# Padding the slots of a split adjacency matrix and the blocks of its features by 32 bytes in a float32r graph kernel

## The chip, the core and the metric

The kernel runs on one core of a Trainium2 chip. The metric is the device time of one execution, in microseconds. Before the change it is 406.56 us, the median of three runs (406.36 to 406.57).

## The reference

`N` is 4096 nodes and `D` is 128 features. Two branches share one adjacency matrix `adj` (4096 x 4096, float32):

```
h   = relu(layernorm(x))                      # 4096 x 128
for (feat, eps, W, b) in ((h, eps1, W1, b1), (x2, eps2, W2, b2)):
    ax = adj @ feat
    y  = ax + (1 + eps) * ax
    for i in range(3):
        y = relu(y @ W[i].T + b[i])
out = x + concat(y1, y2) @ Wm.T + bm
```

Nearly all of the arithmetic is in the two products with `adj`.

## The kernel before

**Split operands.** TensorE is given float32r operands. To keep float32 accuracy each operand is split into a high part (a rounded copy) and a low part (what the rounding lost). A product is then three matmuls into the same PSUM bank: low features with high adjacency (L587), high features with high adjacency (L588), high features with low adjacency (L591). The features are the stationary operand (128 columns, loaded by LDWEIGHTS), and the adjacency is the moving operand (512 columns). The function `product` writes this, and `aggregate` and `opening_aggregate` call it for every block. The first units of the kernel use `passes` (L605) and `norm_aggregate` (L633, L638) for the same three products in another order, and the branch of `x2` uses plain float32 matmuls on unsplit data for its first two units (L619).

**Tiling.** The output is made in 8 chunks of 512 columns. A chunk needs 8 units of the adjacency. A unit is 128 partitions by 2048 columns, which are 4 blocks (`j`) of 512 columns (2048 bytes) each. A unit is used for both branches: 4 blocks x 2 branches x 3 matmuls are 24 matmuls. There are 64 units in all.

**Staging.** `adj_raw`, `adj_hi` and `adj_lo` are rings of 4 slots; unit `u` of a chunk stands in slot `u % 4`. SyncE's queue loads a unit of 1 MB into `adj_raw`, ScalarE copies it to `adj_hi` (L277), VectorE subtracts to make `adj_lo` (L447), and TensorE reads `adj_hi` and `adj_lo`. Units are fed back by the semaphore `unit_used`. The features are split once, in the opening (L319, L343 and L353 on ScalarE for `feat_hi`, L246 and L253 on GpSimd for `feat_lo`), and stay in `feat_hi` and `feat_lo`, [128, 2 branches, 32 blocks, 128], for the whole kernel.

**Layers.** Between the units of a chunk TensorE does the layers of the chunk before (`branch_layer`, `merge`), again with `product`: the stationary operand is a block of `w_lo` or `w_hi`, the moving operand is `act_hi` or `act_lo`. Their output goes to `hidden` and `merged`. The last chunk's late branch does its layers in quarters, with plain float32 (L733, L739).

**Order.** The order on each engine is written out by hand, program loops included; no planner and no pool decides it. Tensors take SBUF in the order in which they are declared, each start rounded up to 32 bytes.

**Where operands start.** The build places `adj_hi` at byte 49280, `adj_lo` at 82048, `feat_hi` at 114816, `feat_lo` at 147584, `w_hi` at 201152, `w_lo` at 205248, `act_hi` at 213600 and `act_lo` at 217696 of each partition. `adj_raw` (16512) and `x2_rows` (188544), the operands of the plain float32 matmuls, stand beside them. Counted modulo 512 bytes (a stationary block is 128 x 4 = 512 bytes long), every block of the adjacency, split or raw, and every block of the features and of `x2_rows` begins at 128, every block of `w_hi` and `w_lo` at 448, and both halves of `act_hi` and `act_lo` at 96.

Of the kernel before, what the change touches and what calls it, by code (L numbers as in the profile page):

```python
# [6 lines left out]
def gnn_layer_kernel(nc, adj_tiles, adj_first, adj_second, x_tiles, x2_tiles, x_t, w_t, bias_t, eps, out_t):  # L7
# [3 lines left out]
    F32R = mybir.dt.float32r  # L11
# [8 lines left out]
    CHUNKS = N // CW  # L20
    U = UNITS_ALL // CHUNKS
    BLOCKS = N // P
    RING = 4
    LAYERS = 3
    STEPS = LAYERS + 1
# [45 lines left out]
    with ExitStack() as ctx:  # L71
# [8 lines left out]


        adj_raw = sb("adj_raw", [P, RING, UNIT_COLS])
        adj_hi = sb("adj_hi", [P, RING, UNIT_COLS], F32R)
        adj_lo = sb("adj_lo", [P, RING, UNIT_COLS], F32R)

        feat_hi = sb("feat_hi", [P, 2, BLOCKS, D], F32R)
        feat_lo = sb("feat_lo", [P, 2, BLOCKS, D], F32R)

        x_rows = sb("x_rows", [P, X_SLOTS, JB, D])
# [74 lines left out]
        def f32(ap):  # L164
            return ap.bitcast(F32)
# [73 lines left out]
        @block.gpsimd  # L239
        def _(pool):  # L240

            def low_of_x2(u):
                rows = slice(u * JB, (u + 1) * JB)
                pool.wait_ge(x2_loaded[u % X_SLOTS], 16 * (u // X_SLOTS + 1))
                pool.wait_ge(feat2_hi_made, x2_count(u))
                nc.gpsimd.tensor_tensor(feat_lo[:, 1, rows, :], x2_rows[:, u % X_SLOTS], f32(feat_hi[:, 1, rows, :]),  # L246
                                        ALU.subtract).then_inc(feat2_lo_made, 1)

            def low_of_x(u):
                rows = slice(u * JB, (u + 1) * JB)  # L250
                pool.wait_ge(feat1_hi_made, u + 1)
                pool.wait_ge(relu_made, u + 1)
                nc.gpsimd.tensor_tensor(feat_lo[:, 0, rows, :], x_rows[:, u % X_SLOTS], f32(feat_hi[:, 0, rows, :]),  # L253
                                        ALU.subtract).then_inc(feat1_lo_made, 1)

            low_of_x(0)
            for u in range(1, U):
                low_of_x2(u)
                low_of_x(u)
                if u == 1:  # L260
                    low_of_x2(0)
            pool.dma_start(x_res[:, :], x_t[:, 0:CW]).then_inc(res_loaded, 16)


            with pool.Fori(0, CHUNKS - 1) as c:
                pool.wait_ge(y_made, c + 1)
                pool.dma_start(out_t[:, bass.ds(c * CW, CW)], y_sb[:, :]).then_inc(out_stored, 16)  # L267
                pool.wait_ge(out_stored, 16 * (c + 1))
                pool.dma_start(x_res[:, :], x_t[:, bass.ds(c * CW + CW, CW)]).then_inc(res_loaded, 16)
            pool.wait_ge(out_stored, 16 * (CHUNKS - 1))  # L270

        @block.scalar
        def _(act):
            def high_of_unit(c, u):
                act.wait_ge(raw_loaded[u % RING], 16 * (c * (U // RING) + (u // RING + 1)))
                act.wait_ge(unit_used, c * U + (u + 1 - RING))
                nc.scalar.activation(adj_hi[:, u % RING, :], adj_raw[:, u % RING, :], ACT.Copy).then_inc(hi_made, 1)  # L277

            def source(m, k, b):

# [30 lines left out]
            def high_of_opening(s):  # L311
                act.wait_ge(raw_loaded[s % RING], 16 * (s // RING + 1))
                if s >= RING:
                    act.wait_ge(unit_used, s + 1 - RING)
                nc.scalar.activation(adj_hi[:, s % RING, :], adj_raw[:, s % RING, :], ACT.Copy).then_inc(hi_made, 1)  # L315

            def high_of_x2(u):
                act.wait_ge(x2_loaded[u % X_SLOTS], 16 * (u // X_SLOTS + 1))
                nc.scalar.activation(feat_hi[:, 1, u * JB:(u + 1) * JB, :], x2_rows[:, u % X_SLOTS],  # L319
                                     ACT.Copy).then_inc(feat2_hi_made, 1)  # L320

            def std_of_x(u):
# [12 lines left out]
            def rectify_half(h, rectified, rounded):  # L335

                blocks = slice(h * HALF, (h + 1) * HALF)
                for j in range(blocks.start, blocks.stop):
                    xs = x_rows[:, 0, j, :]
                    last = nc.scalar.activation(xs, xs, ACT.Relu, bias=shift[:, j:j + 1], scale=rstd[:, j:j + 1])  # L340
                last.then_inc(rectified, 1)
                act.wait_ge(rectified, 1)
                nc.scalar.activation(feat_hi[:, 0, blocks, :], x_rows[:, 0, blocks, :], ACT.Copy).then_inc(rounded, 1)  # L343

            def rectify(u):

                act.wait_ge(rstd_made, u + 1)
                for j in range(JB):
                    xs = x_rows[:, u % X_SLOTS, j, :]
                    last = nc.scalar.activation(xs, xs, ACT.Relu, bias=shift[:, j:j + 1], scale=rstd[:, j:j + 1])  # L350
                last.then_inc(relu_made, 1)
                act.wait_ge(relu_made, u + 1)
                nc.scalar.activation(feat_hi[:, 0, u * JB:(u + 1) * JB, :], x_rows[:, u % X_SLOTS],  # L353
                                     ACT.Copy).then_inc(feat1_hi_made, 1)


# [77 lines left out]
        def _(dve):  # L434
# [8 lines left out]
            def low_of_unit(c, u):  # L443
                dve.wait_ge(raw_loaded[u % RING], 16 * (c * (U // RING) + (u // RING + 1)))
                dve.wait_ge(hi_made, c * U + (u + 1))
                dve.wait_ge(unit_used, c * U + (u + 1 - RING))
                nc.vector.tensor_tensor(adj_lo[:, u % RING, :], adj_raw[:, u % RING, :], f32(adj_hi[:, u % RING, :]),  # L447
                                        ALU.subtract).then_inc(lo_made, 1)

            def low_of_branch(m, k, b):  # L450
# [51 lines left out]
            def low_of_opening(s):  # L502
                dve.wait_ge(raw_loaded[s % RING], 16 * (s // RING + 1))
                dve.wait_ge(hi_made, s + 1)
                if s >= RING:
                    dve.wait_ge(unit_used, s + 1 - RING)
                nc.vector.tensor_tensor(adj_lo[:, s % RING, :], adj_raw[:, s % RING, :], f32(adj_hi[:, s % RING, :]),  # L507
                                        ALU.subtract).then_inc(lo_made, 1)

            nc.vector.memset(zero[:, :], 0.0).then_inc(zero_made, 1)  # L510
# [72 lines left out]
        def _(pe):  # L583
# [16 lines left out]
            def passes(out, s, b, passes_of, start=False):  # L600
                u = OPENING[s][0]
                for k, (feat, adj) in enumerate(passes_of):
                    for j in range(JB):
                        slot, cols = columns(s, j)
                        last = nc.tensor.matmul(out[:, :], feat[:, b, u * JB + j, :], adj[:, slot, cols],  # L605
                                                start=start and k == 0 and j == 0, stop=False)
                return last

# [14 lines left out]
            def norm_aggregate():  # L623

                for h in range(2):
                    pe.wait_ge(feat1_hi_made if h else half_feat1_made, 1)
                    for s in range(2):
                        out = opening_bank(s, late)
                        whole = s == 0 or h == 1
                        pe.wait_ge(hi_made if whole else fine_hi_made, s + 1 if whole else SECOND_UNIT + 1)  # L630
                        for j in range(h * HALF, (h + 1) * HALF):
                            slot, cols = columns(s, j)
                            nc.tensor.matmul(out[:, :], feat_hi[:, late, j, :], adj_hi[:, slot, cols],  # L633
                                             start=(j == 0), stop=False)
                        pe.wait_ge(lo_made if whole else fine_lo_made, s + 1 if whole else SECOND_UNIT + 1)
                        for j in range(h * HALF, (h + 1) * HALF):
                            slot, cols = columns(s, j)
                            nc.tensor.matmul(out[:, :], feat_hi[:, late, j, :], adj_lo[:, slot, cols],  # L638
                                             start=False, stop=False)
                pe.wait_ge(feat1_lo_made, 1)  # L640
                for s in range(2):
                    signal(0, late, passes(opening_bank(s, late), s, late, [(feat_lo, adj_hi)]))
# [20 lines left out]
            def opening_aggregate(s, b):  # L663
# [5 lines left out]
                pe.wait_ge(feat2_lo_made if b else feat1_lo_made, u + 1)  # L669
                for j in range(JB):  # L670
                    slot, cols = columns(s, j)
                    last = product(out[:, :], feat_hi[:, b, u * JB + j, :], feat_lo[:, b, u * JB + j, :],
                                   adj_hi[:, slot, cols], adj_lo[:, slot, cols],
                                   start=False, stop=(u == U - 1 and j == JB - 1),
                                   lo_ready=(lo_made, s + 1) if j == 0 else None)
# [2 lines left out]
            def aggregate(c, u, b):  # L678
# [4 lines left out]
                pe.wait_ge(hi_made, c * U + (u + 1))  # L683
                for j in range(JB):
                    s, cols = columns(u, j)
                    last = product(acc[b][:, :], feat_hi[:, b, u * JB + j, :], feat_lo[:, b, u * JB + j, :],
                                   adj_hi[:, s, cols], adj_lo[:, s, cols],
                                   start=(u == 0 and j == 0), stop=(u == U - 1 and j == JB - 1),
                                   lo_ready=(lo_made, c * U + (u + 1)) if j == 0 else None)
# [142 lines left out]
```

## Time and profile before

| | |
|---|---|
| median of 3 runs | 406.56 us |
| the profiled execution, its own time | 406.39 us |
| its span, first to last instruction | 404.7 us |
| granted TensorE clock | 1.00 |
| TensorE matmuls busy | 400.2 us, 99% of the span |
| TensorE weight loads busy | 325.4 us, 80% |
| VectorE busy | 219.1 us, 54% |
| ScalarE busy | 219.4 us, 54% |
| GpSimd busy | 30.5 us, 8% |
| read from and written to HBM | 73.93 MB and 2.10 MB |

The span is 1.7 us shorter than the time of the same execution. Busy time of TensorE counts overlapping matmuls once, so 99% says that some matmul was always under way, and not how densely they follow each other. That is read from the distance between the starts of two matmuls, called the pitch below. The duration of one matmul in a row is longer than the pitch, since it includes the way through the array, which overlaps with the next one.

### The profile page before, as it was taken

Reading aid. Unit: us, or ns where it says so; the run is one execution under the profiler, and the core shown is the slowest. Engines: PE = TensorE matmul, PEld = TensorE weight load, DVE = VectorE, ACT = ScalarE, POOL = GpSimd, SP = SyncE. Lnnn points to the kernel's source line nnn. Section 1 sums busy time; section 2 is a strip of 40 time slices with the busy share of each in tenths; the row PEclk is TensorE's granted clock in tenths of the full one; section 3 lists DMA queues with packets and bytes.
Section 4 is the critical chain, followed back from the end, with each engine's and each line's share of the span. In section 5 each row is a group of like instructions: output and inputs, shape, how many; then the busy total and the mean of one; then the engine's idle time right before and its main releaser. Section 6 shows DMA issues by size and latency. Waiting matters only on the chain.

```text
span 404.7 us, 4822 instructions
## 1 busy us (share of the span) xinstructions
PE 400.2 (99%) x1751; PEld 325.4 (80%) x1751; DVE 219.1 (54%) x258; ACT 219.4 (54%) x259; POOL 30.5 (8%) x35
## 2 busy tenths in 40 slices
PE   8999999999999999999999999999999999999997
PEld 2788888888888888888888888888888888888886
DVE  3998887656464434551645517345373444755223
ACT  4877667657564533555433556334565335766034
POOL 0243332100010000000100001000000000000100
DMA  7997786754636165334574336653175550740100
GB/s 303 420 377 285 296 314 238 244 208 160 232 146 210 44 241 205 109 120 191 186 280 164 122 128 236 230 206 141 67 262 204 207 196 38 275 166 2 52 0 28
DMA packets 14029, 76.21 MB, mean 188 GB/s; under 512 B 1920, under 2 KB 2176, under 8 KB 6080
## 3 DMA queue, kind: packets, MB, share of 16 engines
q1 hardware_dynamic: 12240, 71.18, 46.9%
q0 software_dynamic: 1200, 3.93, 2.9%
q10 hardware_dynamic: 576, 0.92, 0.6%
q8 instruction: 9, 0.15, 0.1%
q14 instruction: 4, 0.03, 0.0%
HBM read 73.93 MB, written 2.10 MB: 188 GB/s over the span
## 4 chain that ended last, share of the span: by engine, by line
PE 97%; DMA 2%; ACTq 0%; DVE 0%; issue 0%; DVEq 0%
PE acc L591 24%; PE acc L588 24%; PE acc L587 24%; PE second_acc L587 3%; PE second_acc L591 3%; PE second_acc L588 3%; PE hidden L588 3%; PE hidden L591 3%; PE hidden L587 3%; PE acc L605 2%; PE second_acc L605 2%; DMA adj_raw<-adj_first 2%; PE second_acc L619 1%; PE merged L588 1%; PE merged L591 1%; PE merged L587 1%
## 5 line engine op out<-in xcount | busy, mean ns | idle before, releaser
L588 PE MATMUL acc<-adj_hi,feat_hi 128*128 128x512 f32 x432 | 168.1, 389 | 0.0
L587 PE MATMUL acc<-adj_hi,feat_lo 128*128 128x512 f32 x432 | 168.1, 389 | 0.0
L591 PE MATMUL acc<-adj_lo,feat_hi 128*128 128x512 f32 x432 | 168.0, 389 | 0.0
L447 DVE TENSOR_TENSOR adj_lo<-adj_raw,adj_hi 128x2048 fp32r<-128x2048 f32 x48 | 108.3, 2289 | 36.7 <-ACT adj_hi L277 35.8
L277 ACT ACTIVATE adj_hi<-adj_raw 128x2048 fp32r<-128x2048 f32 x48 | 90.3, 1925 | 16.5 <-PE acc L591 14.6
L453 DVE TENSOR_TENSOR act_lo<-act_f,act_hi 128x512 fp32r<-128x512 f32 x60 | 41.0, 690 | 105.3 <-ACT act_f L297 105.3
L588 PEld LDWEIGHTS acc<-adj_hi,feat_hi 128*128 128x128 f32 x432 | 81.1, 188 | 17.1
L587 PEld LDWEIGHTS acc<-adj_hi,feat_lo 128*128 128x128 f32 x432 | 81.1, 188 | 17.1
L591 PEld LDWEIGHTS acc<-adj_lo,feat_hi 128*128 128x128 f32 x432 | 81.1, 188 | 16.8
L296 ACT ACTIVATE act_hi<-hidden,bias 128x512 fp32r<-128x512 f32 x45 | 30.9, 687 | 96.2 <-PE hidden L591 96.2
L507 DVE TENSOR_TENSOR adj_lo<-adj_raw,adj_hi 128x2048 fp32r<-128x2048 f32 x14 | 31.5, 2289 | 6.5 <-ACT adj_hi L315 6.2
L296 ACT ACTIVATE act_hi<-acc,ax_scale 128x512 fp32r<-128x512 f32 x13 | 8.9, 688 | 46.0 <-PE acc L591 42.8
L297 ACT ACTIVATE act_f<-hidden,bias 128x512 f32<-128x512 f32 x45 | 31.1, 690 | 0.0
L267 POOL DMA_DIRECT2D out_t<-y_sb x7 | 3.8, 546 | 280.6 <-DVE y_sb L465 280.6
L315 ACT ACTIVATE adj_hi<-adj_raw 128x2048 fp32r<-128x2048 f32 x13 | 24.2, 1900 | 0.0
L588 PE MATMUL second_acc<-adj_hi,feat_hi 128*128 128x512 f32 x48 | 18.7, 389 | 0.0
L587 PE MATMUL second_acc<-adj_hi,feat_lo 128*128 128x512 f32 x48 | 18.7, 389 | 0.0
L591 PE MATMUL second_acc<-adj_lo,feat_hi 128*128 128x512 f32 x48 | 18.7, 389 | 0.0
L588 PE MATMUL hidden<-act_hi,w_hi 128*128 128x512 f32 x45 | 17.9, 399 | 0.0
L591 PE MATMUL hidden<-act_lo,w_hi 128*128 128x512 f32 x45 | 17.8, 396 | 0.0
L587 PE MATMUL hidden<-act_hi,w_lo 128*128 128x512 f32 x45 | 17.7, 393 | 0.0
L465 DVE SCALAR_TENSOR_TENSOR y_sb<-merged,bias,x_res 128x512 f32<-128x512 f32 x7 | 5.2, 749 | 21.9 <-PE merged L591 21.9
(91 smaller groups left out, 251.3 us busy)
## 6 DMA issues: line engine op xcount, KB each, us to landing
adj_raw<-adj_tiles SPq DMA_DIRECT2D x62, 1024.0 KB, 5.1
x_rows<-x_tiles SPq DMA_DIRECT2D x15, 256.0 KB, 7.1
x_res<-x_t POOLq DMA_DIRECT2D x8, 256.0 KB, 6.4
out_t<-y_sb POOLq DMA_DIRECT2D x7, 256.0 KB, 2.3
adj_raw<-adj_second SPq DMA_DIRECT2D x2, 512.0 KB, 6.6
adj_raw<-adj_first ACTq DMA_DIRECT2D x2, 256.0 KB, 5.0
adj_raw<-adj_first SPq DMA_DIRECT2D x2, 256.0 KB, 4.7
w_raw<-w_t SPq DMA_DIRECT2D x1, 512.0 KB, 5.8
```

What stands on the lines that cost most here:

```text
L277: nc.scalar.activation(adj_hi[:, u % RING, :], adj_raw[:, u % RING, :], ACT.Copy).then_inc(hi_made, 1)
L296: nc.scalar.activation(act_hi[:, b, :], src[:, :], **how).then_inc(act_hi_made[b], 1)
L297: nc.scalar.activation(act_f[:, b, :], src[:, :], **how).then_inc(act_f_made[b], 1)
L315: nc.scalar.activation(adj_hi[:, s % RING, :], adj_raw[:, s % RING, :], ACT.Copy).then_inc(hi_made, 1)
L447: nc.vector.tensor_tensor(adj_lo[:, u % RING, :], adj_raw[:, u % RING, :], f32(adj_hi[:, u % RING, :]), ALU.subtract).then_inc(lo_made, 1)
L453: nc.vector.tensor_tensor(act_lo[:, b, :], act_f[:, b, :], f32(act_hi[:, b, :]), ALU.subtract).then_inc(act_lo_made[b], 1)
L465: nc.vector.scalar_tensor_tensor(y_sb[:, :], merged[:, :], bias[:, MATS - 2:MATS - 1], x_res[:, :], ALU.add, ALU.add).then_inc(y_made, 1)
L507: nc.vector.tensor_tensor(adj_lo[:, s % RING, :], adj_raw[:, s % RING, :], f32(adj_hi[:, s % RING, :]), ALU.subtract).then_inc(lo_made, 1)
L587: nc.tensor.matmul(out, lhs_lo, rhs_hi, start=start, stop=False)
L588: nc.tensor.matmul(out, lhs_hi, rhs_hi, start=False, stop=False)
L591: return nc.tensor.matmul(out, lhs_hi, rhs_lo, start=False, stop=stop)
L605: last = nc.tensor.matmul(out[:, :], feat[:, b, u * JB + j, :], adj[:, slot, cols], start=start and k == 0 and j == 0, stop=False)
```

## The change

A slot of `adj_hi` and of `adj_lo` grows from 2048 to 2056 elements, and a block of `feat_hi` from 128 to 136 elements. The 8 elements (32 bytes) behind each are never written or read; every access is narrowed to the part used before. `adj_raw`, `feat_lo`, the weights and the activations keep their shapes.

```diff
+    PAD = 8
...
-        adj_hi = sb("adj_hi", [P, RING, UNIT_COLS], F32R)
-        adj_lo = sb("adj_lo", [P, RING, UNIT_COLS], F32R)
-
-        feat_hi = sb("feat_hi", [P, 2, BLOCKS, D], F32R)
+        adj_hi = sb("adj_hi", [P, RING, UNIT_COLS + PAD], F32R)
+        adj_lo = sb("adj_lo", [P, RING, UNIT_COLS + PAD], F32R)
+
+        feat_hi = sb("feat_hi", [P, 2, BLOCKS, D + PAD], F32R)
         feat_lo = sb("feat_lo", [P, 2, BLOCKS, D], F32R)
...
-                nc.scalar.activation(adj_hi[:, u % RING, :], adj_raw[:, u % RING, :], ACT.Copy).then_inc(hi_made, 1)
+                nc.scalar.activation(adj_hi[:, u % RING, 0:UNIT_COLS], adj_raw[:, u % RING, :], ACT.Copy).then_inc(hi_made, 1)
...
-                nc.vector.tensor_tensor(adj_lo[:, u % RING, :], adj_raw[:, u % RING, :], f32(adj_hi[:, u % RING, :]),
+                nc.vector.tensor_tensor(adj_lo[:, u % RING, 0:UNIT_COLS], adj_raw[:, u % RING, :], f32(adj_hi[:, u % RING, 0:UNIT_COLS]),
                                         ALU.subtract).then_inc(lo_made, 1)
...
-                nc.scalar.activation(feat_hi[:, 0, u * JB:(u + 1) * JB, :], x_rows[:, u % X_SLOTS],
+                nc.scalar.activation(feat_hi[:, 0, u * JB:(u + 1) * JB, 0:D], x_rows[:, u % X_SLOTS],
                                      ACT.Copy).then_inc(feat1_hi_made, 1)
...
-                    last = product(acc[b][:, :], feat_hi[:, b, u * JB + j, :], feat_lo[:, b, u * JB + j, :],
+                    last = product(acc[b][:, :], feat_hi[:, b, u * JB + j, 0:D], feat_lo[:, b, u * JB + j, :],
                                    adj_hi[:, s, cols], adj_lo[:, s, cols],
```

The other lines of the diff narrow accesses to `feat_hi`, `adj_hi` and `adj_lo` in the same way. Each engine issues the same instructions in the same order as before.

Placed by the same rule, the tensors now begin at 49280 (`adj_hi`), 82176 (`adj_lo`), 115072 (`feat_hi`), 149888 (`feat_lo`), 203456 (`w_hi`), 207552 (`w_lo`), 215904 (`act_hi`) and 220000 (`act_lo`). Modulo 512 bytes, the operands begin at:

| operand | before | after |
|---|---|---|
| moving, `adj_hi` in slot s | 128 | 128 + 32 s |
| moving, `adj_lo` in slot s | 128 | 256 + 32 s |
| stationary, `feat_hi` block k (0 to 63 over both branches) | 128 | 384 + 32 k |
| stationary, `feat_lo` | 128 | 384 |
| moving, `act_hi` and `act_lo` | 96 | 352 |
| stationary, `w_hi` and `w_lo` | 448 | 192 |

## Rows read from the trace of the kernel before

**Rows 1.** The page's busy time: us, share of the span, instructions.

```profile
PE 400.2 (99%) x1751; PEld 325.4 (80%) x1751; DVE 219.1 (54%) x258; ACT 219.4 (54%) x259; POOL 30.5 (8%) x35
```

**Rows 2.** Waits of TensorE, whole span: us in total, times, longest.

```profile
PE merged L744 <- PEq L826: 1.0, 1, 1.0
PE acc L619 <- DMA adj_raw<-adj_first: 0.5, 2, 0.4
```

**Rows 3.** Groups by line: count, busy us, mean ns of one, idle before.

```profile
L588 PE MATMUL acc<-adj_hi,feat_hi 128*128 128x512 f32 x432 | 168.1, 389 | 0.0
L587 PE MATMUL acc<-adj_hi,feat_lo 128*128 128x512 f32 x432 | 168.1, 389 | 0.0
L591 PE MATMUL acc<-adj_lo,feat_hi 128*128 128x512 f32 x432 | 168.0, 389 | 0.0
...
L588 PE MATMUL hidden<-act_hi,w_hi 128*128 128x512 f32 x45 | 17.9, 399 | 0.0
L591 PE MATMUL hidden<-act_lo,w_hi 128*128 128x512 f32 x45 | 17.8, 396 | 0.0
L587 PE MATMUL hidden<-act_hi,w_lo 128*128 128x512 f32 x45 | 17.7, 393 | 0.0
```

**Rows 4.** Window of aggregation alone, instructions of acc: busy us (count), clock, DMA, GB/s.

```profile
161.57:172.44 10.87, 10.87 (x48) 1.00 0.33 121
```

**Rows 5.** TensorE's timeline: start us, us to the last end, of eight plain float32 matmuls.

```profile
9.27 3.60 PE L619 MATMUL second_acc<-adj_raw,x_rows 128*128 128x512 f32 x8
```

**Rows 6.** The tile second_acc, 9.2 to 12.35 us: ns min/median/max, first and last start.

```profile
L619 PE MATMUL second_acc<-adj_raw,x_rows x8: 592/592/592, 9.3 to 12.3; 128*128 128x512 f32 x8
```

**Rows 7.** Weight loads by line: busy us, mean ns of one.

```profile
L587 PEld LDWEIGHTS acc<-adj_hi,feat_lo 128*128 128x128 f32 x432 | 81.1, 188 | 17.1
L588 PEld LDWEIGHTS hidden<-act_hi,w_hi 128*128 128x128 f32 x45 | 8.5, 188 | 1.9
```

**Rows 8.** TensorE's timeline around a layer: start us, duration us.

```profile
159.94 0.39 PE L591 MATMUL acc<-adj_lo,feat_hi 128*128 128x512 f32 x1
160.16 0.39 PE L587 MATMUL hidden<-act_hi,w_lo 128*128 128x512 f32 x1
160.40 0.40 PE L588 MATMUL hidden<-act_hi,w_hi 128*128 128x512 f32 x1
160.63 0.40 PE L591 MATMUL hidden<-act_lo,w_hi 128*128 128x512 f32 x1
160.87 0.39 PE L587 MATMUL hidden<-act_hi,w_lo 128*128 128x512 f32 x1
161.10 0.40 PE L588 MATMUL hidden<-act_hi,w_hi 128*128 128x512 f32 x1
161.34 0.39 PE L591 MATMUL hidden<-act_lo,w_hi 128*128 128x512 f32 x1
161.57 0.39 PE L587 MATMUL acc<-adj_hi,feat_lo 128*128 128x512 f32 x1
```

**Rows 9.** Groups of the acc matmuls between 387.42 and 389.27 us, behind a single-branch layer.

```profile
L587 PE MATMUL acc<-adj_hi,feat_lo 128*128 128x512 f32 x3 | 1.2, 395 | 0.0
L588 PE MATMUL acc<-adj_hi,feat_hi 128*128 128x512 f32 x3 | 1.2, 394 | 0.0
L591 PE MATMUL acc<-adj_lo,feat_hi 128*128 128x512 f32 x2 | 0.8, 391 | 0.0
```

**Rows 10.** Groups of ScalarE and VectorE that write the padded tensors.

```profile
L447 DVE TENSOR_TENSOR adj_lo<-adj_raw,adj_hi 128x2048 fp32r<-128x2048 f32 x48 | 108.3, 2289 | 36.7 <-ACT adj_hi L277 35.8
L277 ACT ACTIVATE adj_hi<-adj_raw 128x2048 fp32r<-128x2048 f32 x48 | 90.3, 1925 | 16.5 <-PE acc L591 14.6
...
L353 ACT ACTIVATE feat_hi<-x_rows 128x512 fp32r<-128x512 f32 x7 | 4.4, 633 | 0.2
```

More of the change, by code:

```diff
@@ L245, in low_of_x2 @@
                 pool.wait_ge(feat2_hi_made, x2_count(u))
-                nc.gpsimd.tensor_tensor(feat_lo[:, 1, rows, :], x2_rows[:, u % X_SLOTS], f32(feat_hi[:, 1, rows, :]),
+                nc.gpsimd.tensor_tensor(feat_lo[:, 1, rows, :], x2_rows[:, u % X_SLOTS], f32(feat_hi[:, 1, rows, 0:D]),
                                         ALU.subtract).then_inc(feat2_lo_made, 1)
@@ L252, in low_of_x @@
                 pool.wait_ge(relu_made, u + 1)
-                nc.gpsimd.tensor_tensor(feat_lo[:, 0, rows, :], x_rows[:, u % X_SLOTS], f32(feat_hi[:, 0, rows, :]),
+                nc.gpsimd.tensor_tensor(feat_lo[:, 0, rows, :], x_rows[:, u % X_SLOTS], f32(feat_hi[:, 0, rows, 0:D]),
                                         ALU.subtract).then_inc(feat1_lo_made, 1)
@@ L314, in high_of_opening @@
                     act.wait_ge(unit_used, s + 1 - RING)
-                nc.scalar.activation(adj_hi[:, s % RING, :], adj_raw[:, s % RING, :], ACT.Copy).then_inc(hi_made, 1)
+                nc.scalar.activation(adj_hi[:, s % RING, 0:UNIT_COLS], adj_raw[:, s % RING, :], ACT.Copy).then_inc(hi_made, 1)
             def high_of_x2(u):
                 act.wait_ge(x2_loaded[u % X_SLOTS], 16 * (u // X_SLOTS + 1))
-                nc.scalar.activation(feat_hi[:, 1, u * JB:(u + 1) * JB, :], x2_rows[:, u % X_SLOTS],
+                nc.scalar.activation(feat_hi[:, 1, u * JB:(u + 1) * JB, 0:D], x2_rows[:, u % X_SLOTS],
                                      ACT.Copy).then_inc(feat2_hi_made, 1)
@@ L342, in rectify_half @@
                 act.wait_ge(rectified, 1)
-                nc.scalar.activation(feat_hi[:, 0, blocks, :], x_rows[:, 0, blocks, :], ACT.Copy).then_inc(rounded, 1)
+                nc.scalar.activation(feat_hi[:, 0, blocks, 0:D], x_rows[:, 0, blocks, :], ACT.Copy).then_inc(rounded, 1)
             def rectify(u):
@@ L506, in low_of_opening @@
                     dve.wait_ge(unit_used, s + 1 - RING)
-                nc.vector.tensor_tensor(adj_lo[:, s % RING, :], adj_raw[:, s % RING, :], f32(adj_hi[:, s % RING, :]),
+                nc.vector.tensor_tensor(adj_lo[:, s % RING, 0:UNIT_COLS], adj_raw[:, s % RING, :], f32(adj_hi[:, s % RING, 0:UNIT_COLS]),
                                         ALU.subtract).then_inc(lo_made, 1)
@@ L604, in passes @@
                         slot, cols = columns(s, j)
-                        last = nc.tensor.matmul(out[:, :], feat[:, b, u * JB + j, :], adj[:, slot, cols],
+                        last = nc.tensor.matmul(out[:, :], feat[:, b, u * JB + j, 0:D], adj[:, slot, cols],
                                                 start=start and k == 0 and j == 0, stop=False)
@@ L632, in norm_aggregate @@
                             slot, cols = columns(s, j)
-                            nc.tensor.matmul(out[:, :], feat_hi[:, late, j, :], adj_hi[:, slot, cols],
+                            nc.tensor.matmul(out[:, :], feat_hi[:, late, j, 0:D], adj_hi[:, slot, cols],
                                              start=(j == 0), stop=False)
@@ L637, in norm_aggregate @@
                             slot, cols = columns(s, j)
-                            nc.tensor.matmul(out[:, :], feat_hi[:, late, j, :], adj_lo[:, slot, cols],
+                            nc.tensor.matmul(out[:, :], feat_hi[:, late, j, 0:D], adj_lo[:, slot, cols],
                                              start=False, stop=False)
@@ L671, in opening_aggregate @@
                     slot, cols = columns(s, j)
-                    last = product(out[:, :], feat_hi[:, b, u * JB + j, :], feat_lo[:, b, u * JB + j, :],
+                    last = product(out[:, :], feat_hi[:, b, u * JB + j, 0:D], feat_lo[:, b, u * JB + j, :],
                                    adj_hi[:, slot, cols], adj_lo[:, slot, cols],
```

## The prediction

> **What bounds the kernel now.** I read the busy times first. Some matmul is under way in 99% of the span, while VectorE and ScalarE are busy for 54% each [rows 1]. Busy time can hide waits, so the waits of TensorE come second: they are 1.0 us at the start and 0.5 us for the first load, and nothing afterwards [rows 2]. TensorE is the bound from beginning to end, and every nanosecond of its pitch counts once per matmul. Third come the groups by line. The matmuls that read padded tensors are the 1296 into `acc`, 389 ns each [rows 3]; with those into `second_acc` and those of the opening they are 1512. I count them so: 60 units of 24 matmuls are 1440, units 2 and 3 of the opening have 24 each, and units 0 and 1 have 12 each, since their other branch is plain float32.
>
> Fourth is the pitch. In a stretch of aggregation alone, 48 matmuls take 10.87 us, so one starts every 226.5 ns at a granted clock of 1.00, the level of 2.4 GHz [rows 4]. At 2.4 GHz 512 columns alone are 213.3 ns. How low a pitch can the trace show? The eight plain float32 records from 9.27 us on run until 3.60 us later, and each is 592 ns long [rows 5, 6]: (3600 - 592) / 7 is 429.7 ns between starts, which is two passes of 214.9 ns. Those passes read operands that begin at 128 modulo 512 as well, and lose next to nothing. So a float32r matmul loses about 11.6 ns (226.5 - 214.9) somewhere. While it streams, the next weight load of 188 ns reads SBUF beside it [rows 7]. That the two reads get in each other's way is the obvious suspect, and where operands begin is what the change alters.
>
> **What the change costs and brings.** Instruction counts, sizes, waits and order stay, so there is nothing to add on any queue: the DMAs write `adj_raw`, `x_rows` and `x2_rows`, which keep their shapes. What is left is how fast each access runs.
>
> ScalarE and VectorE: the writes of whole slots stay one contiguous run of 2048 elements. Writes of `feat_hi` become four runs of 128, with a gap of 32 bytes, and happen 17 times at 616 to 633 ns in the opening. I cost these edits at nothing. Their cover is that no later matmul waits [rows 2]; were a slot's copy 10% slower (190 ns of 1925, or 230 of 2289 [rows 10]), the feeding of a unit would still take 4.6 us of a 24-matmul unit of 5.4 us (24 x 226.5), so nothing is late next.
>
> TensorE: does the pitch depend on where operands begin? The trace of before has one other pair of operands. A layer's moving operand begins at 96 and its weights at 448, modulo 512, while aggregation has 128 and 128. In the layers the same three instructions last 393, 399 and 396 ns in place of 389, with 0.0 idle [rows 3], and the weight load remains 188 ns [rows 7]. The six matmuls from 160.16 to 161.57 us start 235 ns apart on average, as rows of two decimals have it [rows 8]. The added duration, 4, 10 and 7 ns, mean **7 ns**, is then added pitch. These starts are 160 bytes apart, an odd multiple of 32, whereas aggregation's distance is 0. The step into a layer, where a moving operand at 128 meets weights at 448 (an even multiple of 32 apart), costs nothing: the matmul at 159.94 lasts 390 ns to two decimals and the next starts 220 ns later [rows 8].
>
> There is a second sign. Behind a layer of a single branch, eight aggregation matmuls with exactly the old addresses last 395, 394 and 391 ns, on average 393.6 [rows 9], against 389 in the settled stream. The two reads therefore have a relative timing, too. With offsets that repeat they fall into a good one after some eight matmuls and stay in it. With offsets that change from block to block they are pushed out of it again and again.
>
> Now the sum. In the changed kernel the moving start less the stationary start is, modulo 512, 256 + 32 (s - k) bytes for high with high, 384 + 32 (s - k) for high features with `adj_lo`, and 256 + 32 s for `feat_lo`, where s is the slot and k the block. Each of them is an odd multiple of 32 for half of the combinations. Counting the moving operand alone gives the same number: slots 1 and 3 begin at odd multiples of 32, and they hold 756 of the 1512 matmuls. **756 x 7 ns is 5.3 us.** The other half keeps an even distance, and I take it at 0, as the step into a layer shows. The layers keep their own distance of 160 bytes and their cost. From 406.4 us, the profiled execution's own time, this gives 411.7 us; the median of the runs is 0.2 us above that execution, so the two bases are the same within what counts here.
>
> The bounds of this term: 756 x 4 ns, the least of the layer's three lines, is 3.0 us (409.4). If no matmul finds the good timing any more, 1512 x 4.6 ns [rows 9] is 7.0 us (413.4), and 1512 x 7 ns is 10.6 us (417.0). Below, if the whole loss went away, 1512 x 11.6 ns is 17.5 us (388.9). I take 5.3 us because the layer rows are the only ones in which the start distance differs, and the factor of one half is the same by either count.
>
> **The rivals.** *First, faster.* Two reads that begin at the same place modulo 512 bytes hit the same piece of memory at the same time, and 32 bytes of shift part them. For it speaks the loss of 11.6 ns, which the plain float32 passes don't have although their operands begin at 128 and 128 as well; they stream at half the rate. Against it speak the layers, whose operands are parted and which are slower. If half of the combinations lost all of it, 756 x 11.6 ns is 8.8 us and the time 397.6 us; if a third of the loss went on all, 1512 x 3.9 ns is 5.9 us and the time 400.5 us. It decides as soon as the mean over the 16 possible distances is under 226.5 ns; the trace shows only four of them (moving start less stationary start, modulo 512: 0 in aggregation, 160 in a layer, 192 on entering one, 480 on leaving it).
>
> *Second, no change.* The loss could be fixed for each weight load of float32r, whatever the addresses, and the layers could be slow for a reason of their own, such as the semaphore waits that stand between their matmuls. For it: nothing in the trace shows two float32r streams without the loss. Against it: L588's matmul has no wait in front of it and is the slowest of a layer's three, and aggregation's own waits, at each unit's first block, leave its mean at 389 ns [rows 3]. Then the time is 406.4 us.
>
> The Trainium skill, page "SBUF — State Buffer", section "Who interferes with whom", speaks for this rival: it gives TensorE two independent read ports, one for the moving operand and one for weights, and says that it never waits on anyone. By that rule the starts could not matter and the time would be 406.4 us. The trace disagrees at least in part, since the same instructions take 389 and up to 399 ns. The Trainium skill, page "TensorE: Matmul & The Clock Gate", section "Wait — 56ns, not 53.3ns?", measures a pitch of N / 2.4 GHz plus 2.5 ns, 215.7 ns for 512 columns; the plain float32 passes agree (214.9), aggregation does not (226.5). By that page 10.8 ns per matmul are there to be won, an estimate of 16 us in all, which is the first rival's extreme.
>
> *Third, slower by more:* the stream never settles, at 413.4 us, with 417.0 as the worst. It shares its place with my forecast and differs in its count.
>
> **How the numbers follow.** My forecast, a mixture of settled and disturbed matmuls between 409 and 413 us, gets 0.40, and the never-settled stream 0.15. No change gets 0.15. Faster gets 0.30, since only 4 of 16 distances have been seen and one of them is the coincidence that a shift could cure. A measurement of this kernel can tell 0.2%, 0.8 us, from no change. So slower has 0.55, same 0.15, faster 0.30. The range reaches from 399, which leaves out the deeper half of the first rival, up to 416, which leaves out only the worst bound. The likeliest case's own range is 409.4 to 413.4.
>
> **What would show it.** In the changed profile: if I am right, the groups of `acc` rise from 389 ns to about 392 on average, with single matmuls spread between 389 and 400, slots 1 and 3 or odd distances above the others; the layers stay at 393, 399 and 396; the count of instructions is the same and TensorE's waits stay at 1.5 us. If all matmuls are at 394, the stream never settles. If `acc` is below 389, the starts did collide and I am wrong in sign; the layers, at an unchanged distance, should then stay slow. If all rows are unchanged, the loss belongs to the weight load itself. If waits appear on `adj_hi` or `adj_lo`, I have missed a cost on ScalarE or VectorE.

## The result, and the profile after

The changed kernel takes 414.67 us (median of 4 runs, 414.48 to 414.79), against 406.46 us for the kernel before, run beside it (4 runs). The ratio is 1.020, with a 95% interval from 1.018 to 1.022: 8.2 us slower.

TensorE is still the bound. The page's busy times, and the waits of TensorE (us in total, times, longest), of the changed kernel, beside [rows 1] and [rows 2]:

```profile
PE 408.3 (99%) x1751; PEld 326.2 (79%) x1751; DVE 219.3 (53%) x258; ACT 219.7 (53%) x259; POOL 30.5 (7%) x35
```

```profile
PE merged L748 <- PEq L830: 1.0, 1, 1.0
PE acc L623 <- DMA adj_raw<-adj_first: 0.8, 1, 0.8
```

The waits are 0.3 us longer, ScalarE and VectorE are busy 0.3 and 0.2 us longer, and TensorE is busy 8.1 us longer. The time is in the matmuls themselves. These are the groups by line (count, busy us, mean ns of one, idle before), which answer to [rows 3]; the lines moved by four:

```profile
L595 PE MATMUL acc<-adj_lo,feat_hi 128*128 128x512 f32 x432 | 170.8, 395 | 0.0
L591 PE MATMUL acc<-adj_hi,feat_lo 128*128 128x512 f32 x432 | 170.3, 394 | 0.0
L592 PE MATMUL acc<-adj_hi,feat_hi 128*128 128x512 f32 x432 | 170.3, 394 | 0.0
...
L592 PE MATMUL hidden<-act_hi,w_hi 128*128 128x512 f32 x45 | 17.8, 396 | 0.0
L591 PE MATMUL hidden<-act_hi,w_lo 128*128 128x512 f32 x45 | 17.8, 395 | 0.0
L595 PE MATMUL hidden<-act_lo,w_hi 128*128 128x512 f32 x45 | 17.8, 395 | 0.0
```

The aggregation went from 389 to 394 or 395 ns. The mean rise, 5.3 ns, times the 1512 matmuls that read padded tensors is 8.1 us, nearly all of what was lost. In a stretch of aggregation between two layers, the window with the matmuls into `acc` alone (busy us and count, clock, DMA, GB/s) shows the pitch:

```profile
164.97:176.11 11.14, 11.14 (x48) 1.00 0.33 122
```

That is 232.1 ns from start to start, against 226.5 in [rows 4]. Slots and blocks of either parity are mixed in it, and TensorE's timeline (start, duration) has no second sort of matmul that stays at 389 ns:

```profile
165.21 0.39 PE L592 MATMUL acc<-adj_hi,feat_hi 128*128 128x512 f32 x1
165.44 0.39 PE L595 MATMUL acc<-adj_lo,feat_hi 128*128 128x512 f32 x1
165.67 0.39 PE L591 MATMUL acc<-adj_hi,feat_lo 128*128 128x512 f32 x1
165.90 0.40 PE L592 MATMUL acc<-adj_hi,feat_hi 128*128 128x512 f32 x1
166.13 0.40 PE L595 MATMUL acc<-adj_lo,feat_hi 128*128 128x512 f32 x1
```

Slot 2 and slot 3, one half of this stretch each, do this alike: in either, 17 of the 24 starts that follow a matmul are 230 to 239 ns behind it, and the other 7 are 225 to 229 ns.

### The profile page after: what moved, and what is told of

It reads as the page before. It is cut to its first block, busy times and chain, and to the rows that moved or that the text cites. A ratio compares the mean times of both kernels' runs of the same rounds, so it can differ in the third digit from the quotient of the medians.

```text
span 413.1 us, 4822 instructions
## 1 busy us (share of the span) xinstructions
PE 408.3 (99%) x1751; PEld 326.2 (79%) x1751; DVE 219.3 (53%) x258; ACT 219.7 (53%) x259; POOL 30.5 (7%) x35
## 4 chain that ended last, share of the span: by engine, by line
PE 97%; DMA 1%; DVE 0%; SPq 0%; issue 0%; DVEq 0%
PE acc L595 24%; PE acc L592 24%; PE acc L591 24%; PE second_acc L595 3%; PE second_acc L592 3%; PE second_acc L591 3%; PE hidden L592 3%; PE hidden L591 3%; PE hidden L595 3%; PE acc L609 2%; PE second_acc L609 2%; DMA adj_raw<-adj_first 1%; PE second_acc L623 1%; PE merged L591 1%; PE merged L595 1%; PE merged L592 1%
## 5 line engine op out<-in xcount | busy, mean ns | idle before, releaser
L595 PE MATMUL acc<-adj_lo,feat_hi 128*128 128x512 f32 x432 | 170.8, 395 | 0.0
L591 PE MATMUL acc<-adj_hi,feat_lo 128*128 128x512 f32 x432 | 170.3, 394 | 0.0
L592 PE MATMUL acc<-adj_hi,feat_hi 128*128 128x512 f32 x432 | 170.3, 394 | 0.0
```

The costliest lines, as they stand in the source:

```text
L591: nc.tensor.matmul(out, lhs_lo, rhs_hi, start=start, stop=False)
L592: nc.tensor.matmul(out, lhs_hi, rhs_hi, start=False, stop=False)
L595: return nc.tensor.matmul(out, lhs_hi, rhs_lo, start=False, stop=stop)
```

## The experiments

Two theories stood at first. The **settling theory**: two streams of reads find a good relative timing while their starts repeat, and changing starts keep them out of it, whatever the starts are. The **distance theory**: a given distance between moving and stationary start has its own price.

**One padding at a time.** The first keeps the padded slots and takes the padding off `feat_hi`:

```diff
-        feat_hi = sb("feat_hi", [P, 2, BLOCKS, D + PAD], F32R)
+        feat_hi = sb("feat_hi", [P, 2, BLOCKS, D], F32R)
```

> Only the slots of adj_hi and adj_lo are padded; every block of feat_hi begins at the same place modulo 512 again. Settling theory (the two reads fall into a good relative timing only while the starts repeat, whatever they are): the starts now change once per unit of 24 matmuls, and between adj_hi and adj_lo inside a unit (128 bytes apart in place of 0), so part of the loss returns to before: 408 to 413 us. Distance theory (odd multiples of 32 bytes between the starts cost): slots 1 and 3 are bad as a whole, half of the 8.2 us or more, with acc matmuls of two sorts, 389 ns in slots 0 and 2 and 400 ns in slots 1 and 3.

Measured: 413.89 us, ratio 1.019 (1.017 to 1.020). The second pads only `feat_hi`:

```diff
-        adj_hi = sb("adj_hi", [P, RING, UNIT_COLS + PAD], F32R)
-        adj_lo = sb("adj_lo", [P, RING, UNIT_COLS + PAD], F32R)
+        adj_hi = sb("adj_hi", [P, RING, UNIT_COLS], F32R)
+        adj_lo = sb("adj_lo", [P, RING, UNIT_COLS], F32R)
```

> Only the blocks of feat_hi are padded; the slots of the adjacency begin at the same place again. Settling theory: the stationary start changes with every block, and between feat_lo and feat_hi, so nothing settles and the whole 8.2 us remain: 413.5 to 415.5 us. Distance theory: odd blocks are bad, even ones good, about 410 to 411 us.

Measured: 413.11 us, ratio 1.017 (1.015 to 1.018). Each half alone costs most of the whole (7.5 and 6.7 of 8.2 us), so they don't add. Neither theory had both numbers. The first kernel is above the settling theory's range; the distance theory's "half of the 8.2 us or more" allows it. The second is a little under the settling theory's range and well above the other's. The two sorts of slots that the distance theory wanted are looked up below, with the table of distances.

**A constant distance.** The kernel before, with one spacer:

```diff
+        spacer = sb("spacer", [P, 8])
         feat_hi = sb("feat_hi", [P, 2, BLOCKS, D], F32R)
```

> No padding; one spacer of 32 bytes in front of feat_hi shifts feat_hi, feat_lo and all that stands behind them, so that every block of the features begins 32 bytes off every block of the adjacency, always the same. Settling theory: starts repeat, the stream settles, 406 to 408 us. Distance theory (odd multiple of 32 bytes costs, repeated or not): 1512 x 5 to 7 ns, 414 to 417 us.

Measured: 416.05 us, ratio 1.024 (1.022 to 1.025), with nothing padded and every start repeating. Its slowest group of `acc` (the other two are at 395 ns), and eight of the plain float32 records of its opening (start, us to the last end):

```profile
L592 PE MATMUL acc<-adj_lo,feat_hi 128*128 128x512 f32 x432 | 171.0, 396 | 0.0
...
9.39 3.60 PE L620 MATMUL second_acc<-adj_raw,x_rows 128*128 128x512 f32 x8
```

This is slower than the changed kernel. The settling theory, which wanted 406 to 408 us, falls in the form in which I stated it: repeating is not enough, the distance itself has a price. The plain float32 matmuls don't pay it: the spacer puts `x2_rows` 32 bytes off `adj_raw` as well, and eight of their records still take 3.60 us, as in [rows 5].

**The price of every distance.** A kernel that holds only such matmuls:

```
for i in range(16): 24 x matmul(bank, wts[0], mov[i])     # moving starts 32 bytes apart
for i in range(16): 24 x matmul(bank, wts[i], mov[0])     # stationary starts 32 bytes apart
for i in reversed(range(16)): 24 x matmul(bank, wts[i], mov[i])
```

> Computes nothing of the reference: it writes zeros and runs only float32r matmuls of 512 columns, 24 in a row for each pair of starts, one loop over 16 moving starts 32 bytes apart with one stationary start, one over 16 stationary starts, one with both shifted together. Settling theory: each run of 24 goes through some uneven matmuls of 389 to 400 ns and then stays at one value, whatever the distance. Distance theory: settled values differ by distance, odd multiples of 32 bytes above even ones. If some distance settles well under 389 ns, there is a placement that beats both kernels.

TensorE's timeline of this kernel, one row for each 24 matmuls (start, us to the last end). The letter is the multiple of 32 bytes:

```profile
25.30 5.77 PE L53 MATMUL bank<-mov_b,wts_a 128*128 128x512 f32 x24
30.91 5.67 PE L53 MATMUL bank<-mov_c,wts_a 128*128 128x512 f32 x24
36.41 5.77 PE L53 MATMUL bank<-mov_d,wts_a 128*128 128x512 f32 x24
42.02 5.76 PE L53 MATMUL bank<-mov_e,wts_a 128*128 128x512 f32 x24
47.62 5.78 PE L53 MATMUL bank<-mov_f,wts_a 128*128 128x512 f32 x24
53.24 5.76 PE L53 MATMUL bank<-mov_g,wts_a 128*128 128x512 f32 x24
58.84 5.76 PE L53 MATMUL bank<-mov_h,wts_a 128*128 128x512 f32 x24
64.44 5.63 PE L53 MATMUL bank<-mov_i,wts_a 128*128 128x512 f32 x24
69.91 5.77 PE L53 MATMUL bank<-mov_j,wts_a 128*128 128x512 f32 x24
...
153.62 5.61 PE L56 MATMUL bank<-mov_a,wts_i 128*128 128x512 f32 x24
159.07 5.75 PE L56 MATMUL bank<-mov_a,wts_j 128*128 128x512 f32 x24
...
269.32 5.63 PE L59 MATMUL bank<-mov_c,wts_c 128*128 128x512 f32 x24
274.79 5.63 PE L59 MATMUL bank<-mov_b,wts_b 128*128 128x512 f32 x24
```

Start to start, divided by 24, is the pitch. For moving start less stationary start it reads:

| distance, bytes | 32 | 64 | 96 | 128 | 160 | 192 | 224 | 256 |
|---|---|---|---|---|---|---|---|---|
| ns | 233.8 | 229.2 | 233.8 | 233.3 | 234.2 | 233.3 | 233.3 | 227.9 |

The letter `j` (288) repeats `b`, so the table has a period of 256 bytes. Shifting both operands by 32 bytes changes nothing: `mov_c,wts_c` lasts 5.47 us to the next start, as does `mov_i,wts_a` (5.47, the 227.9 above). These runs hold a few uneven matmuls at their beginning; the run `mov_a,wts_i`, which follows `mov_a,wts_h`, has 5.45 us or 227.1 ns. By the nanoseconds of the trace, of which the rows show two decimals of a microsecond, the first 23 of its 24 pitches are 226.7 ns on average, the settled value for distance 0. So only the distance modulo 256 counts here, 0 is the best of the eight, 64 costs about a third of the others' price, and odd against even is not the rule: 128 and 192 bytes cost as much as 32. The mean of the eight, with 226.7 for distance 0, is 232.2 ns. No start in 32-byte steps goes below the settled pitch of the kernel before.

**Which stationary operand counts.** In the timeline the weight load of the next matmul starts together with the matmul before it. These rows show where `wts_i` gives way to `wts_j` at one and the same moving operand, and where `mov_a` gives way to `mov_b` at one and the same weights:

```profile
158.83 0.40 PE L56 MATMUL bank<-mov_a,wts_i 128*128 128x512 f32 x1
158.83 0.42 PEld L56 LDWEIGHTS bank<-mov_a,wts_j 128*128 128x128 f32 x2
159.07 0.39 PE L56 MATMUL bank<-mov_a,wts_j 128*128 128x512 f32 x1
...
25.08 0.39 PE L53 MATMUL bank<-mov_a,wts_a 128*128 128x512 f32 x1
25.30 0.40 PE L53 MATMUL bank<-mov_b,wts_a 128*128 128x512 f32 x1
```

The last matmul on `wts_i` is at distance 0 from its own weights and already takes 235 ns to the next start, as do the last ones on `wts_a`; the last one with `mov_a` still takes 227 ns, and the first one with `mov_b` 235. So at these steps a matmul's moving start is held against the stationary start of the matmul behind it. It is not so at every distance: the last aggregation matmul before a layer, 192 bytes off the layer's weights, takes 0.22 us [rows 8], where 192 costs 233.3 ns in a row.

**The first two kernels by the table.** With the slots padded alone, slot s has the distances 32 s, 32 s and 128 + 32 s for its three matmuls. The table then gives 228.9, 233.9, 230.6 and 233.6 ns for slots 0 to 3. These rows are the first matmuls of the unit in slot 0, of the one in slot 1, and of the layer behind it:

```profile
151.81 0.40 PE L591 MATMUL acc<-adj_hi,feat_lo 128*128 128x512 f32 x1
157.31 0.40 PE L591 MATMUL acc<-adj_hi,feat_lo 128*128 128x512 f32 x1
162.91 0.39 PE L591 MATMUL hidden<-act_hi,w_lo 128*128 128x512 f32 x1
```

A unit has 24 matmuls, so the pitches are 229.2 and 233.3 ns. Over the 40 units of the third to seventh chunk the trace has 230.3, 233.3, 231.2 and 233.3 ns for slots 0 to 3. So there are two sorts of slots, the odd ones slower, and the table has all four within 1.4 ns. Its total, 1512 times 5.1 ns, is 7.7 us, against 7.5 measured. For the padded features alone it gives 5.5 us (a third of the matmuls at 0, the rest over all eight distances), against 6.7: 1.2 us too little. I worked both out afterwards; they were not forecast.

**Three tests of the table on the real kernel.** The kernel before had distance 0 in all of its aggregation and 160 in its layers. The first test moves the layers to 0 as well:

```diff
+        to_weights = sb("to_weights", [P, 48])
         w_raw = sb("w_raw", [P, MATS, D])
...
+        to_acts = sb("to_acts", [P, 24])
         act_f = sb("act_f", [P, 2, CW])
```

> The kernel before with two spacers (192 bytes before w_raw, 96 before act_f), so that w_hi, w_lo, act_hi and act_lo begin at 128 modulo 256 like adjacency and features. Distance table of the probe (pitch set by the moving start less the next stationary start, modulo 256): all float32r matmuls are now at distance 0 and 226.7 ns; the 177 of the layers fall from about 233.5, 1.2 us, and the uneven matmuls behind single-branch layers lose another 0.1 us: 405.1 us, layer groups at 389 ns. Theory that the layers are slow for their waits or their data, not their starts: unchanged, 406.4 us, and 393 to 399 ns.

Measured: 405.04 us (10 runs), ratio 0.997 (0.996 to 0.998), against 405.1 expected and 406.35 us for the kernel before, run beside it. The groups by line of this kernel:

```profile
L589 PE MATMUL acc<-adj_hi,feat_lo 128*128 128x512 f32 x432 | 168.0, 389 | 0.0
...
L589 PE MATMUL hidden<-act_hi,w_lo 128*128 128x512 f32 x45 | 17.5, 389 | 0.0
L590 PE MATMUL hidden<-act_hi,w_hi 128*128 128x512 f32 x45 | 17.5, 389 | 0.0
L593 PE MATMUL hidden<-act_lo,w_hi 128*128 128x512 f32 x45 | 17.5, 389 | 0.0
```

The layers fell from 393, 399 and 396 ns [rows 3] to 389. The waits (2.0 us in all, against 1.5) and the data are not less than they were, so the theory that these made the layers slow is out, and this kernel beats both others, for 288 bytes of SBUF.

The second test pads the slots by 256 bytes and leaves `feat_hi` as it was:

```diff
-    PAD = 8
+    PAD = 64
```

> As the padding of the adjacency slots alone, but by 256 bytes in place of 32. The starts change with every slot as before, by 256 bytes. Distance table: every distance stays 0 modulo 256, so 406.4 us and acc at 389 ns. Settling theory (any change of starts costs): like the 32-byte padding of the slots, about 413.9 us.

Measured: 406.31 us, ratio 1.000 (0.999 to 1.001), `acc` at its old duration:

```profile
L592 PE MATMUL acc<-adj_hi,feat_hi 128*128 128x512 f32 x432 | 168.1, 389 | 0.0
```

The starts change with every slot, as in the first experiment, and it costs nothing. The two differ in the size of the padding alone and lie 7.6 us apart. The third test is the spacer with 64 bytes in place of 32:

> A spacer of 64 bytes in front of feat_hi in place of 32: features stand 64 bytes behind the adjacency, so the moving start less the stationary is -64, that is 192 modulo 256. Distance table: 233.3 ns, 1512 x 6.6 = 10 us, 416.4 us, as with 32. If only odd multiples of 32 cost, 406 to 410 us.

Measured: 416.36 us, ratio 1.025 (1.023 to 1.026). An even multiple of 32 costs as much as an odd one, as 192 in the table says.

**Finer steps, narrower operands, bfloat16.** The same kind of kernel, with one wide moving tensor whose first column is chosen:

```
for e in range(64): 24 x matmul(bank, wts, mov[:, e:e + 512])
then 384 and 256 moving columns; 96, 64 and 32 stationary columns (e = 0, 8, 16 each); bfloat16 (e = 0, 16, 32)
```

> Computes nothing of the reference: zeros are written, and float32r matmuls run 24 at a time for 64 moving starts 4 bytes apart, then with 384 and 256 moving columns, with stationary operands of 96, 64 and 32 columns, and with bfloat16 operands. If reads collide by pieces of 32 bytes, the pitch changes in steps with the 8 starts inside a piece; if something finer counts, a start between two multiples of 32 bytes may lie below 226.7 ns. If the loss is that of the weight load's reads, 226.7 falls toward 215 ns in proportion to the stationary columns, the loss per matmul stays the same with fewer moving columns, and bfloat16, whose reads are half as wide, loses little or nothing.

Its groups by form (count, busy us, mean ns), whole span:

```profile
L55 PE MATMUL bank<-mov,wts 128*32 128x512 f32 x72 | 16.8, 394 | 0.0
L55 PE MATMUL bank<-mov,wts 128*64 128x512 f32 x72 | 16.7, 392 | 0.0
L55 PE MATMUL bank<-mov,wts 128*128 128x512 bf16 x70 | 15.4, 379 | 0.1
L55 PE MATMUL bank<-mov,wts 128*128 128x384 f32 x72 | 12.6, 335 | 0.0
L55 PE MATMUL bank<-mov,wts 128*128 128x256 f32 x72 | 8.7, 281 | 0.0
```

and around two single starts, 28 bytes (49.9 to 55.3 us) and 20 bytes (38.6 to 44.2 us), a neighbor's few matmuls included:

```profile
L55 PE MATMUL bank<-mov,wts 128*128 128x512 f32 x26 | 6.1, 388 | 0.0
```

```profile
L55 PE MATMUL bank<-mov,wts 128*128 128x512 f32 x25 | 6.2, 404 | 0.0
```

Start to start these runs give the pitches themselves. Two expectations held. The loss does not shrink in proportion to the moving columns: 384 columns have a pitch of 173.3 ns, 13 ns over the 160 that one column per cycle takes at 2.4 GHz, 256 columns 118 to 120 ns, 11 to 13 over 107, and 512 columns at distance 0 have 13 ns as well. And bfloat16 loses little, 215.8 ns against 213.3. Two failed. There are no steps of 32 bytes: within the first piece the durations go from 388 to 404 ns. And a stationary operand of 32 columns in place of 128 is no faster, 394 ns, although its weight load takes 108 ns in place of 190. So the loss that stays at distance 0 is not simply the number of weight reads. Among the 64 starts of the 128 x 512 matmul nothing goes below it: the best reach 388 ns, a pitch of 226.7, which is the settled pitch again.

The other shapes say how far the table reaches, and it is not far. Each was run at distances of 0, 32 and 64 bytes. With 384 moving columns the pitch is 173.3 to 173.5 ns at all three, and with bfloat16 215.8 at the two whose end is in the trace (379 ns long at all three): no price for the distance. With 256 columns 0 is the dearest, 119.6 ns against 118.0 and 117.9. With 64 stationary columns 64 bytes are the best (228.5 ns against 230.0 at 0), and with 32 columns the three differ by less than 1 ns (231.2 at 0). With 96 stationary columns 32 bytes are the best (226.6 ns), as the groups at distances 0, 32 and 64 show:

```profile
L55 PE MATMUL bank<-mov,wts 128*96 128x512 f32 x23 | 5.5, 392 | 0.0
...
L55 PE MATMUL bank<-mov,wts 128*96 128x512 f32 x22 | 5.1, 389 | 0.0
...
L55 PE MATMUL bank<-mov,wts 128*96 128x512 f32 x23 | 5.5, 395 | 0.0
```

So the table, and with it the advice to let both operands start alike, is shown for 128 stationary by 512 moving columns of float32r and for nothing else.

**Is the price one per matmul, without memory?** The pattern of `product`, with the start of the low stationary (i.e. `wts[k]`) and the low moving operand (`mov[i]`) varied:

```
10 x (matmul(bank, wts[k], mov[0]); matmul(bank, wts[0], mov[0]); matmul(bank, wts[0], mov[i]))   for i, k in 8 x 8
```

> Computes nothing of the reference: zeros are written, and triples of float32r matmuls run in the pattern of the kernel's product (low weights with high moving, high with high, high weights with low moving), ten triples for each of 8 starts of the low moving operand by 8 starts of the low stationary one, 32 bytes apart, modulo 256. The distance table without memory predicts for each triple the mean of three entries: with the low stationary operand shifted alone, one matmul of three leaves 226.7 ns; it is the one before the shifted weights if the next stationary operand counts, and the shifted one itself if its own counts. If the state is carried along, means differ from the table. Any triple under 3 x 226.7 = 680 ns would be a better layout for the kernel; I expect none.

TensorE's timeline, first with all starts equal, then with `wts_b` as the low stationary operand:

```profile
18.56 0.39 PE L54 MATMUL bank<-mov_a,wts_a 128*128 128x512 f32 x1
...
19.24 0.39 PE L54 MATMUL bank<-mov_a,wts_a 128*128 128x512 f32 x1
...
24.79 0.39 PE L54 MATMUL bank<-mov_a,wts_b 128*128 128x512 f32 x1
25.02 0.40 PE L55 MATMUL bank<-mov_a,wts_a 128*128 128x512 f32 x1
25.25 0.40 PE L56 MATMUL bank<-mov_a,wts_a 128*128 128x512 f32 x1
25.49 0.39 PE L54 MATMUL bank<-mov_a,wts_b 128*128 128x512 f32 x1
```

Equal starts give 0.68 us for a triple. With the low stationary operand shifted by 32 bytes it is 0.70 us, where the table by itself gives 2 x 226.7 + 233.5 = 687 ns: more than one matmul suffers. The group of the middle matmul over all 64 combinations says the same:

```profile
L55 PE MATMUL bank<-mov_a,wts_a 128*128 128x512 f32 x640 | 252.9, 395 | 0.0
```

It has the same two tensors each time, and the stationary operand that follows it is the same too. Yet it lasts 395 ns on average, because of neighbors whose starts differ. So there is memory, and a mixed pattern is not the mean of the table's entries. No combination is under 0.68 us, as expected, but equal starts are not the only one to reach it: the low weights shifted by 128 bytes with the low moving operand shifted by 160 (`wts_e`, `mov_f`) give 0.68 us too. Most of the others lie between 0.69 and 0.70.

## Why the prediction was right, and where it was not

**Direction and range.** Slower was forecast at 0.55, within 399 to 416 us. 414.67 is inside, near the upper end. It is above 409.4 to 413.4, the likeliest case's own range: that case (a mixture of settled and disturbed matmuls, 0.40) did not come, and what the range covered it with was the rival of a stream that never settles (0.15). The named signs say the same: `acc` was to rise to about 392 ns with slots 1 and 3 above the others, and it rose to 394 and 395, with a pitch of 232.4, 233.1, 232.3 and 231.8 ns in slots 0 to 3 (third to seventh chunk). The sign and the price were reasoned; that the number fell into the range in spite of the wrong count was in part luck.

**Steps that held.** The bound is TensorE's pitch with no waits, and stayed it. The costs set at nothing on ScalarE and VectorE were nothing (0.3 and 0.2 us of busy time, with no waits for them). The reading that decided the sign was that a layer's matmuls are slower because of where their operands start; the alignment experiment shows this directly, 393 to 399 ns turning into 389. The price taken from them, 7 ns, is about that of most distances: the constant shifts of 32 and 64 bytes cost 9.7 and 10.0 us over 1512 matmuls, 6.4 and 6.6 ns each.

**The step that failed** is the count: "Each of them is an odd multiple of 32 for half of the combinations", and for the other half "I take it at 0, as the step into a layer shows". One single matmul at an even distance was no base for it: in a row, that same distance of 192 bytes costs 6.6 ns, as the spacer of 64 bytes shows with 10.0 us. Six of the eight distances in the table cost 6.6 to 7.5 ns, 64 bytes cost 2.5, and only 0 is free. The term is 1512 times about 5.4 ns (8.2 us), not 756 times 7 ns (5.3 us), and 411.7 was 3.0 us too low.

**The third rival**, a stream that never settles on all 1512 matmuls at 4.6 ns more (413.4 us), had the right count and nearly the right price. It had only part of the reason. That changing starts cost something by themselves is false, since 256 bytes of padding are free; what the last kernel of matmuls alone confirms is that a deviating distance also disturbs matmuls beside it. Two thirds of the matmuls go through the eight distances equally (232.2 ns). The rest have 0, 32, 64 and 96 bytes if a matmul's own weights count and 128 to 224 if the next ones do, and the table's sum is 7.7 us or 9.0 us. The 8.2 measured lie between; the table can't say more closely, because of its neighbors' effect. What the padding did was to leave the one distance in eight that was free.

**The first rival**, that equal starts collide and a shift parts them, is refuted for the matmuls of this kernel: equal starts are the best of the eight distances in steps of 32 bytes, and none of 64 starts in steps of 4 bytes goes below them. It is not refuted for every shape, since 96 stationary or 256 moving columns were faster with a shift of 32 bytes. **The second rival**, no change, is refuted with it, and so is the rule of the Trainium skill, page "SBUF — State Buffer", section "Who interferes with whom", so far as it would make the starts of TensorE's operands a matter of no consequence: by it the time was 406.4 us, by measurement 414.67. Whether the two read ports are independent is not decided by that, since the runs don't say that reads are what wait.

**What stays open** is the mechanism. Why 256 bytes, why the loss depends on the start irregularly below 32 bytes, why the good distance is another with 96 stationary columns and there is none with 384 moving ones, and what the 11 ns are that a float32r matmul of 512 columns takes over a bfloat16 one (226.7 and 215.8), was not settled. A clash of the weight load with the moving reads is a guess that fits a matmul being slowed by the weights behind it, and no run shows it: a load of a quarter of the width did not help.

## What to carry to other kernels

With back-to-back float32r matmuls of 128 stationary by 512 moving columns, let the moving and the stationary operands begin at the same place modulo 256 bytes, layers and small weights included; look up the addresses that the allocator gave, and round slot strides to 256 bytes. For other shapes try a few distances first, since the runs with fewer stationary or fewer moving columns don't follow this rule. Padding to spread addresses is not free and should be tried on one pair of operands by itself first. Rows of the kernel before that differ only in their tensors' places (here 389 against 399 ns for the same instruction) are worth more than an expectation of how a memory conflicts; but one row gives a price, not the share of matmuls that pay it.

## What the runs showed that I had not expected

- The pitch depends on the distance with a period of 256 bytes, and has one good value among eight in steps of 32 bytes: 226.7 ns at 0, 229 at 64, 233 to 234 at the others. It holds for 128 x 512 alone of the shapes tried.
- A loss of 11 to 13 ns per float32r matmul for 256, 384 and 512 moving columns, which a weight load of 32 columns in place of 128 does not lower.
- Plain float32 matmuls did not change with a shift of 32 bytes between their operands (eight records in 3.60 us, as before).
- 288 bytes of spacers make this tuned kernel 1.3 us faster (405.04 us).
